# Loading layer 0's weights of a two-layer recurrent kernel by partition halves, with rows of 8 KB, ahead of everything else

## The reference

```
for each layer l in (0, 1):
    xW = x @ Wx + b                       # (8, 1024, 512), all steps at once
    h  = cond_1024                        # (8, 512), the same start for both layers
    for t in range(1024):
        h = tanh(h @ Wh + xW[:, t]);  hs[:, t] = h
    x = x + hs                            # layer 1 reads this sum
return x
```

## Time and profile before

| | us |
|---|---|
| median of 3 runs (lowest, highest) | 2063.53 (2063.33, 2063.71) |
| the profiled execution's own time | 2062.76 |
| its span, first to last instruction | 2060.9 |
| TensorE matmul busy in the span | 2045.6 (99%) |
| VectorE, ScalarE, GpSimd busy | 1750.8, 1280.4, 446.9 |
| bytes read from HBM, written | 37.90 MB, 16.78 MB |

### The profile page before, as it was taken

How to read it: one execution, slowest core, us unless ns; L and a number is a source line. 1 busy time by engine, 2 the same in 40 slices (tenths; PEclk the granted TensorE clock), 3 DMA queues, 4 the chain that set the end, 5 groups by cost and what they waited for, 6 DMA issues and landing times.

```text
span 2060.9 us, 219225 instructions
## 1 busy us (share of the span) xinstructions
PE 2045.6 (99%) x98444; PEld 1864.0 (90%) x98444; DVE 1750.8 (85%) x10243; ACT 1280.4 (62%) x6660; POOL 446.9 (22%) x2061
## 2 busy tenths in 40 slices
PE   8999999999999999999999999999999999999998
PEld 6999999999999999999999999999999999999997
DVE  5888888888888888888888888888888888888887
ACT  3666666666666666666666666666666666666664
POOL 3222222222222222222222222222222222222221
PEclk9999999999999999999999999999999999999999
DMA  3000000000000000000000000000000000000000
GB/s 108 24 27 24 28 24 27 24 27 24 28 24 27 24 27 24 28 23 28 24 27 24 27 24 27 24 27 24 27 24 27 25 26 25 26 25 26 25 26 15
DMA packets 112537, 56.35 MB, mean 27 GB/s; under 512 B 12496, under 2 KB 111072, under 8 KB 112096
## 3 DMA queue, kind: packets, MB, share of 16 engines
q1 hardware_dynamic: 111456, 53.53, 8.9%
q10 hardware_dynamic: 864, 1.18, 0.2%
q0 software_dynamic: 32, 0.02, 0.0%
HBM read 37.90 MB, written 16.78 MB: 27 GB/s over the span
## 4 chain that ended last, share of the span: by engine, by line
PE 99%; DVE 0%; DMA 0%; issue 0%; ACT 0%; SPq 0%; ACTq 0%
PE ps_rec L246 44%; PE ps_rec L263 33%; PE ps_xw L223 22%; DMA wh<-wh_in 0%; DVE zt L434 0%; DVE z L441 0%; ACT h L357 0%; SPq L189 0%; SPq L191 0%; SPq L187 0%; DVE x_out L472 0%; ACTq L58 0%
## 5 line engine op out<-in xcount | busy, mean ns | idle before, releaser
L246 PE MATMUL ps_rec<-wh,h 128*32 128x128 f32 x32912 | 1259.7, 273 | 8.1 <-ACT h L357 6.9
L357 ACT ACTIVATE h<-z 128x24 f32<-128x24 f32 (+1 forms) x4096 | 659.7, 208 | 685.9 <-DVE z L441 644.1
L263 PE MATMUL ps_rec<-wh_part,h 128*32 128x128 bf16 x48960 | 1041.4, 219 | 1.2 <-issue 1.2
L246 PEld LDWEIGHTS ps_rec<-wh,h 128*32 128x32 f32 x32912 | 878.1, 109 | 35.1 <-ACT h L357 11.3
L263 PEld LDWEIGHTS ps_rec<-wh_part,h 128*32 128x32 bf16 x48960 | 726.8, 96 | 151.3 <-issue 1.5
L180 POOL TENSOR_TENSOR h<-h 128x16 f32<-128x16 f32 x2039 | 432.5, 212 | 1602.9 <-DVE h L180 1602.9
L441 DVE TENSOR_REDUCE z<-zt 128x24 f32<-128x72 f32 (+1 forms) x4096 | 668.7, 205 | 70.2 <-DVE zt L434 0.6
L351 ACT ACTIVATE ps_rec<-ps_xw,mask 128x128 f32<-128x128 f32 x2048 | 664.1, 324 | 78.0 <-PE ps_xw L223 78.0
L434 DVE STREAM_TRANSPOSE zt<-ps_rec 128x128 f32<-128x128 f32 x2048 | 649.0, 317 | 17.8 <-PE ps_rec L263 10.4
L180 DVE TENSOR_TENSOR h<-h 128x16 f32<-128x16 f32 x2041 | 357.5, 175 | 210.4 <-ACT h L357 1.4
L223 PE MATMUL ps_xw<-wx,x_mid 128*32 128x128 f32 x8192 | 403.7, 273 | 1.6 <-issue 1.6
(11 more groups left out here) (19 smaller groups left out, 12.4 us busy)
## 6 DMA issues: line engine op xcount, KB each, us to landing
x_pe<-x_t SPq DMA_DIRECT2D x256, 64.0 KB, 2.0
x_dve<-x_t SPq DMA_DIRECT2D x256, 64.0 KB, 1.9
out_t<-x_out SPq DMA_DIRECT2D x256, 64.0 KB, 1.5
wh<-wh_in SPq DMA_DIRECT2D x1, 1024.0 KB, 4.7
wx<-wx_in SPq DMA_DIRECT2D x1, 1024.0 KB, 8.1
wx<-wx_in ACTq DMA_DIRECT2D x2, 256.0 KB, 5.5
wx<-wx_in SPq DMA_DIRECT2D x2, 256.0 KB, 5.3
wh<-wh_in SPq DMA_DIRECT2D x2, 256.0 KB, 7.1
```

What stands on the lines that cost most here:

```text
L246: mm = pe.matmul(rows(ps_rec[l][n % 2], g), h_step(l, n - 1)[:, k, :], wh[l][:, k, g * P:(g + 1) * P], start=False, stop=k == KC - 1 and n ...
L263: mm = pe.matmul(rows(ps_rec[l][n % 2], g), h_bits(l, n - 1)[:, k, :], wh_part[l][:, i, at:at + P], start=False, stop=k == KB[l] - 1 and i ...
L357: act.activation(h_of(l, n)[:, tiles, :], z[l][n % 2][:, :].rearrange("p (k b) -> p k b", k=KC)[:, tiles, :], ACT.Tanh).then_inc(h_count(l ...
```

## The change

The eight 256 KB loads of layer 0's weights become four loads of 512 KB: a weight tile's partitions 0 to 63 on the SP queue, 64 to 127 on the ScalarE queue, all four blocks of a partition in one row of 8 KB. wx[0]'s halves stand first in both queues, ahead of the first x chunk and of bias 0. There are two semaphores for each tile instead of four; TensorE waits for both halves of wx[0] before block 0 of the first projection, then projects all four blocks with no warm rounds between them, runs 5 warm rounds, and waits for both halves of wh[0] before the first recurrence. The warm rounds are (12, 5) instead of (10, 3, 3). GpSimd too waits for both halves of wh[0] before it makes the parts of block 0.

```diff
-WARM = (10, 3, 3)
+WARM = (12, 5)
+PARTITIONS = (slice(0, P // 2), slice(P // 2, P))
...
-        s_wx0 = [sem(f"wx0_loaded{k}") for k in range(KC)]
+        s_wx0 = [sem(f"wx0_loaded{i}") for i in range(2)]
-        s_wh0 = [sem(f"wh0_loaded{k}") for k in range(KC)]
+        s_wh0 = [sem(f"wh0_loaded{i}") for i in range(2)]
...
+            half = PARTITIONS[0]
+            sp.dma_start(wx[0][half, :, :], weights[0][0][half, :, :]).then_inc(s_wx0[0], DMA)
             sp.dma_start(x_pe[0][:, :], x[:, 0, :]).then_inc(x_first[0], DMA)
-            for k in (0, 2):
-                sp.dma_start(wx[0][:, k, :], weights[0][0][:, k, :]).then_inc(s_wx0[k], DMA)
-            for k in (0, 2):
-                sp.dma_start(wh[0][:, k, :], weights[0][1][:, k, :]).then_inc(s_wh0[k], DMA)
+            sp.dma_start(wh[0][half, :, :], weights[0][1][half, :, :]).then_inc(s_wh0[0], DMA)
             sp.dma_start(x_pe[1][:, :], x[:, 1, :]).then_inc(x_first[1], DMA)
...
-                    if (l, n) == (0, 0):
-                        pe.wait_ge(s_wh0[k], DMA)
-                    elif k == KC - 1:
+                    if k == KC - 1 and (l or n):
                         pe.wait_ge(*h_count(l, n - 1))
...
             pe.wait_ge(s_seed, 1)
+            for e in s_wx0:
+                pe.wait_ge(e, DMA)
             for k in range(KC):
-                pe.wait_ge(s_wx0[k], DMA)
                 project(0, 0, k)
-                if k % 2:
-                    warm(ps_rec[1][1], WARM[k // 2 + 1])
+            warm(ps_rec[1][1], WARM[1])
+            for e in s_wh0:
+                pe.wait_ge(e, DMA)
             recur_whole(0, 0)
...
+            half = PARTITIONS[1]
+            act.dma_start(wx[0][half, :, :], weights[0][0][half, :, :]).then_inc(s_wx0[1], DMA)
             act.dma_start(bias[0][:, :], weights[0][2]).then_inc(s_bias[0], DMA)
-            for k in (1, 3):
-                act.dma_start(wx[0][:, k, :], weights[0][0][:, k, :]).then_inc(s_wx0[k], DMA)
-            for k in (1, 3):
-                act.dma_start(wh[0][:, k, :], weights[0][1][:, k, :]).then_inc(s_wh0[k], DMA)
+            act.dma_start(wh[0][half, :, :], weights[0][1][half, :, :]).then_inc(s_wh0[1], DMA)
             act.dma_start(bias[1][:, :], weights[1][2]).then_inc(s_bias[1], DMA)
...
             for l in LAYERS:
+                for e in (s_wh1,) if l else s_wh0:
+                    pool.wait_ge(e, DMA)
                 for k in range(KB[l]):
-                    pool.wait_ge(s_wh0[k] if l == 0 else s_wh1, DMA)
```

## The result

| | before | changed |
|---|---|---|
| median of 15 runs each, us | 2063.33 | 2067.25 |
| profiled execution, us (span) | 2062.76 (2060.9) | 2067.16 (2065.3) |
| first transpose of step 0, us | 11.01 | 14.82 |
| wh of layer 0 complete, us | 10.2 to 10.4 | 13.4 to 13.6 |

I had forecast 2062.8 us in a range of 2061.9 to 2064.0; the time is outside. The rival "half the ports", with a transpose at 14.7 and 2067.2 us, is what came.

A forecast was written before the change was run, and what follows sets the result against it. The prediction took matmuls alone to bound the loop. wh at 9.2 us, 0.05 to the first load and 1.15 of matmuls gave a transpose at 10.4; it took 0.7 us gained: 2063.53 - 0.7 = 2062.8 us, range 2061.9 to 2064.0.

The forecast's parts named there:

- half the ports: Weight loads: each queue writes only 64 partitions, two transfers share 212 GB/s, transpose 3.7 us late, 2067.2 us; chance 0.12.
- Bounds of the kernel and how a shift travels: Whole kernel: the loop is bound by matmuls alone; a shift before the first recurrence moves all that follows equally.
- the code pieces: Between 27 and 56 us: five "issue" pieces of 0.45 to 0.82 us move with the start; 0.4 us allowed either way.
- Transfer of the weights: Layer 0's weight loads: fewer issues, earlier start and steady rate of 423 GB/s land wh at 9.2 us instead of 10.4.
- The terms of that sum: wh's landing: 0.75 start, 2.2 fixed, 2.24 MB at 423 GB/s (5.3), giving 8.3, plus 0.9 slow beginning, 9.2 us.
- The slow beginning: Loads from 3 to 5 us: 209 instead of 375 GB/s, taken as a cold start that costs 0.9 us.
- wx, bias and x: Before the first projection: wx lands at 5.8 to 6.7 us, bias activation adds 0.3, so 6.1 to 7.0 us.
- Warm rounds: TensorE before step 0: twelve end at 6.8 to 7.15 us, five more at 8.8 to 9.1, near wh's landing.
- The split by block: First recurrence: 32 instead of 16 matmuls lie behind wh's last landing, 1.15 instead of 0.75 us, costing 0.4 us.
- Later users: Layer 1's loads and parts: issued 1.2 us earlier, move forward more than their use; slack hides GpSimd's later start.

The follow-up runs named there:

- Experiments 2: Changed kernel with partition halves kept, each half tile loaded by four DMAs with rows of 2 KB; 2066.33 us, ratio 1.0016.
- experiment 3: Changed kernel with even partitions on the SP queue and odd ones on the ScalarE queue, 64 rows of 8 KB per DMA; 2062.43 us, ratio 0.9997.
- experiment 5: Changed kernel with its four half loads issued one after the other, each when the one before has landed; 2076.49 us, ratio 1.0065.
- experiment 4: Changed kernel with each weight tile in one 1 MB DMA over all partitions, 8 KB rows, both on the SP queue; 2062.41 us, ratio 0.9997.
- experiment 1: Changed kernel's four loads cut into block halves (4 KB rows, all 128 partitions) instead of partition halves; 2062.07 us against 2062.56 before, ratio 0.9995.
- Experiment 7: Kernel before with wx's 2 KB-row blocks issued ahead of x chunk 0 and bias 0; 2063.15 us against 2063.00, ratio 1.0001.
- experiment 9: Against experiment 1: wh again by block in 2 KB rows, a wait ahead of each block, warm rounds (12, 4); 2062.24 us against 2063.00 before.
- experiments 8: Against experiment 1: block halves with 4 KB rows kept, but x chunk 0 and bias 0 first in the queues; 2062.31 us, ratio 0.9997.

## Why the prediction was wrong, step by step

**Bounds of the kernel and how a shift travels: right.** Between the profiles the transpose moved by 3.81 us and the medians by 3.92. The allowance of 0.4 us for the code pieces was too small for a single profile; the table shows about 1.

**Transfer of the weights: this step failed.** It read: "because row size and issue order are those of that row". wh[1]'s row was the right row length on the wrong set of partitions: its DMA writes all 128. Priced at 423 GB/s, the 2.24 MB were to take 5.3 us; the loads ran at 196 to 258 GB/s in stretches of 2 us from 3 to 13 us, and wh landed at 13.4 instead of 9.2. Experiments 2, 3 and 5 show that a DMA of one contiguous half is the cause.

**The terms of that sum: two errors that cancel.** The bytes were too few. In the kernel before, 2.53 MB had moved by 10.4 us, not 2.24: x chunk 1, bias 1 and VectorE's x chunks, issued behind wh, moved beside it. In experiment 4 it was 2.55 MB by 9.25 us, some 0.7 us more at 423 GB/s. The slow beginning, for which the sum had 0.9 us, did not come there (408 GB/s from 3 to 5 us). So 9.25 against 9.2 confirms the level of the rate for whole tiles, but the closeness is luck.

**The rival had the right size and the wrong chance.** From the earlier trace rows it worked out wh at 13.5, the transpose at 14.7 and 2067.2 us; measured were 13.4 to 13.6, 14.82 and 2067.25. Its mechanism was right; that it hit so closely is partly luck, since its bytes and its rate were both too low: 2.55 MB had moved by 13.4 us, which from the same 2.95 us on is 244 GB/s, not 212. I gave it 0.12 because two queues side by side had shown no loss. But those transfers wrote all partitions, so they bore no witness on the point at issue. A mechanism that no row contradicts, with a written rule in its favour, deserved at least an even chance. It would then have been the forecast, or the range would have reached it.

The rule was in the Trainium skill, "SBUF — State Buffer", section "Can I just issue two DMAs to hit both halves?", which says that two such DMAs gain 6% over one; here they reached 218 to 258 GB/s in stretches where both queues carried weights (9 to 11 us of the two profiles of the changed kernel), 2 to 21% over one alone at 213. The same page, section "Door 1: The DMA port swizzle", has 196 GB/s for a whole transfer of 1 MiB to one half; the 213 here is the rate in flight. Where the first of the two says that only a transfer spanning all 128 partitions reaches every port, experiment 3 differs: two DMAs of 64 rows, on even and on odd partitions, ran at 406 GB/s together, and the measurement decides.

**wx, bias and x: right as a risk, wrong in size.** I put the bias activation at 6.1 to 7.0 us. With half the rate it ran at 9.20, and TensorE waited 3.10 us for it, hidden under wh. With full-rate loads it ran at 6.44 in experiment 1 and 7.13 in experiment 3, near the forecast. Experiment 7 shows the same move not hidden.

**Warm rounds.** I had the twelve end at 6.8 us if fast, 7.15 if slow. They ended at 6.5 and 7.2 in the two profiles of the changed kernel and at 7.0 and 5.9 in the two of the block halves, so their length is not the kernel's own. In the changed kernel they left gaps of 3.10 and 2.45 us, with the clock at half in or behind them. With full-rate loads a gap of 0 to 1.1 us is left (none in experiment 1, 1.08 us in its second profile, 0.96 in experiment 3), not none as forecast. The five rounds then end at 9.0 to 9.1 us in both profiles of the block halves, as forecast, within 0.1 us of wh's landing. They leave nothing to gain from a faster load.

**The split by block.** Its price, 0.4 us of matmuls behind the last landing, is confirmed in experiment 9, and so is what I left out: 2 KB rows give the same 0.4 us back.

**Later users.** Layer 1's loads moved with wh[0] and nothing waited for them, as forecast.

**Is there a version that beats both?** Against the changed kernel, yes: experiments 1, 3, 4, 8 and 9 all start 3.9 to 4.6 us sooner. Against the kernel before, the block halves were 0.49 and 1.05 us lower by their medians in two comparisons, in line with a start 0.7 to 0.8 us sooner; each interval holds 1, so it isn't proved. The pieces behind the start take some of it back in the profiles: 4.4 and 5.0 us in the block halves, 3.3 in the kernel before.

## What to carry to other kernels

When a load is cut in two for two queues, cut it along the free dimension, not the partitions: the same bytes in four DMAs of the same size landed at 13.4 to 13.6 us by partition halves and at 9.0 by block halves. If it has to be cut by partition, interleave (even and odd, 9.7 us in one profile) rather than halve. And when a load is priced from another row of the trace, check that both agree in partitions as well as in bytes and row length, and count the bytes from the DMA view, not from the order of the issues.

## What the runs showed of the hardware that I had not expected

- One DMA to partitions 0 to 63 alone: 213 GB/s with all 16 DMA engines busy; two such DMAs on the two halves: 218 to 258 GB/s; on even and odd partitions: 406.
- From 3 to 5 us, loads with 2 KB rows behind those of x and bias ran at 209 GB/s in two profiles; with 4 KB rows in that place 360, with 4 or 8 KB rows at the head of the queues (experiments 1, 3 and 4) 406 to 416, with 2 KB rows at the head 324. Why is open.
- TensorE's granted clock fell from 1.00 to 0.50 at the end of the gap of 3.10 us that the warm rounds left (0.85 from 8.5 to 9 us, 0.50 from 9). Behind the gap of 2.45 us in the second profile, and one of 2.01 in experiment 7, it fell only after the matmuls had resumed, and the lower level then held for some 3 us. Behind the gaps of 0.96 us in experiment 3 and 1.08 us in the second profile of the block halves the 32 matmuls took their full-clock 1.08 us.
- Why two queues on different halves do not add up is open: no run here shows which DMA engine writes which partitions, nor whether the limit is on the side of the partitions or of the rows in HBM.
